# Mixture-of-experts stage on Trainium2: gate and up contracted over 128 rows, then over the two 64-row halves of the array, with the remainder's weights streamed per tile

## What is computed

```python
xf = x.reshape(N, Dv)                       # N = 3072 tokens, Dv = 192, layernormed
logits = xf @ router_w.T
top_logits, top_idx = jax.lax.top_k(logits, 2)
top_w = jax.nn.softmax(top_logits, axis=-1)
for e in range(8):
    w_e = jnp.sum(top_w * (top_idx == e), axis=-1)
    h = jax.nn.silu(xf @ Wg[e].T) * (xf @ Wu[e].T)     # 192 -> 768, twice
    out = out + h @ Wd[e].T * w_e[:, None]             # 768 -> 192
```

## Time and profile before

| | |
|---|---|
| median of 3 runs | 2037.2 us (2034.75 to 2037.57) |
| the profiled execution, own time | 2037.6 us |
| its span in the trace | 2035.9 us |
| Mamba program | 0 to about 1513.5 us |
| routing, first gathers | 1513.5 to 1561 us |
| the 55 tiles | 1561 to 2036 us |
| TensorE busy over the span | 1523.3 us (75%) |
| VectorE busy over the span | 1514.1 us (74%) |

### The profile page before, as it was taken

The page is one execution under the profiler, slowest core; times in us unless marked ns, Lnnn a source line. Parts: engine busy times, 40 slices in busy tenths (PEclk is TensorE's granted clock), DMA queues, the critical chain, the costliest instruction groups (busy, mean ns, idle before and its releaser), DMA issues. The chain is left out here.

```text
span 2035.9 us, 19521 instructions
## 1 busy us (share of the span) xinstructions
PE 1523.3 (75%) x4714; PEld 866.1 (43%) x4715; DVE 1514.1 (74%) x1780; ACT 861.1 (42%) x1848; POOL 1056.5 (52%) x539
## 2 busy tenths in 40 slices
PE   6566776776677677767767775876643899999997
PEld 4233343343344334434433443443332566666665
DVE  3699999999999999999999999999954122222221
ACT  2555545554554555455455454554510222222221
POOL 2465676675667657655675675548600233333332
PEclk8777897888788778878878887888875999999999
DMA  3412303031231303122130402213025411111111
GB/s 80 148 48 79 119 29 136 21 129 52 85 114 35 136 16 133 38 99 97 53 120 18 147 37 100 85 42 136 0 73 133 114 26 24 25 24 24 26 24 22
DMA packets 49182, 144.71 MB, mean 71 GB/s; under 512 B 13118, under 2 KB 26028, under 8 KB 48332
## 3 DMA queue, kind: packets, MB, share of 16 engines
q1 hardware_dynamic: 36956, 129.61, 18.7%
q0 software_dynamic: 12144, 14.30, 4.2%
HBM read 132.67 MB, written 11.21 MB: 71 GB/s over the span
## 5 line engine op out<-in xcount | busy, mean ns | idle before, releaser
L629 POOL TENSOR_TENSOR ring<-dtu,brep 128x1536 f32<-128x1536 f32 x192 | 661.0, 3447 | 446.0 <-DVE states L640 316.3
L652 PE MATMUL py<-ring,ident 128*128 128x384 f32 x1536 | 637.2, 568 | 133.7 <-DVE yg L669 110.5
L640 DVE TENSOR_TENSOR_SCAN states<-states,ring 128x768 f32<-128x768 f32 x384 | 673.7, 1755 | 30.2 <-ACT states L616 14.7
L652 PEld LDWEIGHTS py<-ring,ident 128*128 128x128 f32 x1536 | 332.7, 223 | 420.6 <-issue 186.2
L616 ACT ACTIVATE states<-dt_,aneg 128x376 f32<-128x376 f32 x768 | 406.1, 560 | 0.0
L642 DVE TENSOR_TENSOR ring<-states,crep 128x768 f32<-128x768 f32 x384 | 367.6, 957 | 13.2
L613 ACT ACTIVATE states<-zero_cols 128x16 f32<-128x16 f32 x384 | 71.2, 186 | 642.7 <-DVE ring L642 637.6
L1288 PE MATMUL gu<-w,xsT 96*128 x660 | 298.3, 602 | 7.2 <-issue 6.6
L462 PE MATMUL pf<-xT,wxz 97*128 97x384 f32 (+1 forms) x384 | 183.7, 624 | 139.0 <-ACT xT L449 55.3
L1329 DVE COPY yidx<-place 128x1 int32 (+1 forms) x56 | 8.4, 153 | 250.8 <-DMA out_tokens<-ys,yidx 250.8
L1288 PEld LDWEIGHTS gu<-w,xsT 96*128 96x128 f32 x660 | 122.6, 193 | 145.6 <-issue 145.6
(11 more groups left out here) (221 smaller groups left out, 1412.3 us busy)
## 6 DMA issues: line engine op xcount, KB each, us to landing
brep<-b_c_rows SPq DMA_DIRECT2D x64, 768.0 KB, 4.1
crep<-b_c_rows SPq DMA_DIRECT2D x64, 768.0 KB, 4.6
w<-in_w SPq DMA_DIRECT2D x8, 1152.0 KB, 14.2
wd<-in_wd SPq DMA_DIRECT2D x8, 576.0 KB, 16.3
ptok<-in_p_tok SPq DMA_DIRECT2D x8, 384.0 KB, 3.8
pT<-in_p_T SPq DMA_DIRECT2D x8, 384.0 KB, 4.8
out_tokens<-h SPq DMA_DIRECT2D x8, 288.0 KB, 2.1
x_scratch<-x SPq DMA_DIRECT2D x8, 288.0 KB, 2.9
```

Source lines behind the costliest of these rows:

```text
L629: gp.tensor_tensor(ring[:, w % NRING], dtu[:, d, o, :].unsqueeze(1).to_broadcast([128, GN, T]), brep[:, ng], ALU.mult).then_inc(dbu_ok, 1)
L640: v.tensor_tensor_scan(h_in, h_in, x_in, 0.0, ALU.mult, ALU.add).then_inc(scan_ok, 1)
L652: mm = pe.matmul(py[:, 0:T], ident[:], ring[:, w % NRING, i, :], start=(ng == 0 and i == 0), stop=False)
```

## The change

1. The contraction over 192 features is cut as 128 + 64 instead of 96 + 96. For the first 128 rows there are four matmuls on the full array (512 and 256 columns, for gate and for up). For the last 64 rows gate uses partitions 0 to 63 and up partitions 64 to 127: matmuls of 64 rows, 512 columns of gate, 512 of up, 256 of gate, 256 of up.
2. For that the tile's features 128 to 191 must stand on both halves. The table's rows grow to XR + E = 264 floats, SP stores features 128 to 191 a second time per chunk, the second transpose takes 128 columns, and the gather moves 1056 B a row instead of 800.
3. `w13` becomes 128 partitions by 49152 B (768 KB an expert instead of 1152). The weights of the last 64 rows are loaded for each tile into one of two buffers `rest` (`sp_rest`, 384 KB a tile, on SP's queue, its expert number read by SP). It waits until gate/up of tile j-2 is done. `pe_gu` waits for it between its two parts.
4. On SP's queue the loads for tiles 0 and 1 stand ahead of expert 2's weights, those for tiles 2 to 5 behind the weights of expert 7, the others in a loop.
5. Gate and up start on PSUM banks of their own (`gu` grows to 4 banks); `cnt` shares its bank with `yps`.

```diff
-XW = D + E
+XR = 256
+XW = XR + E
@@ norm_x3, and SP's wait at the program's end
-            wait(eng, x3_out, 16 * c)
+            wait(eng, x3_out, 32 * c)
@@ sp_store
             sp.dma_start(rows_of(rows, c), src[:]).then_inc(done, 16)
+            if what == "x3":
+                sp.dma_start(rows_of(dram["x3"][:, D:XR], c), x3[:, :, 128:D]).then_inc(x3_out, 16)
@@ build_experts
-        w13 = sb("w13", [KH, E, 2, 2 * HF])
+        w13 = sb("w13", [128, E, 2 * HF])
+        rest = sb("rest", [128, 2, HF])
-        xsT = sb("xsT", [KH, 2, 2, 128])
+        xsT = sb("xsT", [128, 2, 2, 128])
-        gu = pb("gu", [128, 2 * HF])
+        gu = pb("gu", [128, 2048])
+        gate_up = [gu[:, 1024 * i:1024 * i + HF] for i in range(2)]
-        cnt = pb("cnt", [128, 512])
+        cnt = yps
@@ pe_xT
-            for k in range(2):
-                mm = pe.transpose(xps[0:KH, 128 * k:128 * k + 128], xs[:, b, KH * k:KH * k + KH], ident[:])
-            mm.then_inc(xt_ps, 1)
+            pe.transpose(xps[:, 0:128], xs[:, b, 0:128], ident[:])
+            pe.transpose(xps[:, 128:256], xs[:, b, 128:XR], ident[:]).then_inc(xt_ps, 1)
@@ new
+        def sp_rest(sp, j, b):
+            wait(sp, gu_ok, j - 1)
+            if not isinstance(j, int):
+                alone(sp)
+            e = sp.value_load(owner[0:1, bass.ds(j, 1)], min_val=0, max_val=E - 1)
+            sp.dma_start(rest[:, b, :], a["w13_rest"][:, bass.ds(e, 1), :].rearrange("p a n -> p (a n)")).then_inc(rest_in[b], 16)
@@ pe_gu
-            for n in range(3):
-                for k in range(2):
-                    mm = pe.matmul(gu[:, 512 * n:512 * n + 512], xsT[:, b, k, :], w13[:, bass.ds(e, 1), k, 512 * n:512 * n + 512].rearrange("p a n -> p (a n)"), start=(k == 0), stop=(k == 1))
+            pieces = ((0, 512), (512, HF))
+            for i in range(2):
+                for lo, hi in pieces:
+                    pe.matmul(gate_up[i][:, lo:hi], xsT[:, b, 0, :], w13[:, bass.ds(e, 1), HF * i + lo:HF * i + hi].rearrange("p a n -> p (a n)"), start=True, stop=False)
+            pe.wait_ge(rest_in[b], 16 * (n + 1))
+            for lo, hi in pieces:
+                for i in range(2):
+                    rows = slice(64 * i, 64 * i + 64)
+                    mm = pe.matmul(gate_up[i][:, lo:hi], xsT[rows, b, 1, :], rest[rows, b, lo:hi], start=False, stop=True)
             mm.then_inc(gu_ok, 1)
@@ SP's queue
             for c in range(NCH):
                 sp.dma_start(rows[c], row_w[:, NT * c:NT * c + NT, :]).then_inc(weights_out, 16)
+            sp.wait_ge(rv.sem, rv.after("owner", 0))
+            sp_rest(sp, 0, 0)
+            sp_rest(sp, 1, 1)
             weights(2)
             for b in range(2):
                 sp.wait_ge(xs_in[b], 16)
             for e in range(3, E):
                 weights(e)
+            for j in range(2, HEAD):
+                sp_rest(sp, j, j % 2)
+            with sp.Fori(0, (NJ - HEAD - 1) // 4) as i:
+                for r in range(4):
+                    sp_rest(sp, 4 * i + HEAD + r, r % 2)
+            sp_rest(sp, LAST, LAST % 2)
```

More of the change, by code:

```diff
@@ L1055, in _ @@
             sp.wait_ge(h2_out, 16 * NCH)
-            sp.wait_ge(x3_out, 16 * NCH)
+            sp.wait_ge(x3_out, 32 * NCH)
             sp.wait_ge(filled, 32)
@@ L1229, in build_experts @@
         xs_in = [sem(f"slot_tile_loaded{b}") for b in range(2)]
+        rest_in = [sem(f"rest_weights_loaded{b}") for b in range(2)]
         xt_ps = sem("slot_tile_transposed")
@@ L1280, in act_xT, with pe_gu @@
             wait(act, gu_ok, j - 1)
-            act.activation(xsT[:, b].rearrange("p k t -> p (k t)"), xps[0:KH, 0:256], ACT.Copy).then_inc(xt_sb, 1)
-        def pe_gu(pe, j, b, e):
+            act.activation(xsT[:, b].rearrange("p k t -> p (k t)"), xps[:, 0:256], ACT.Copy).then_inc(xt_sb, 1)
+        def sp_rest(sp, j, b):
[4 more added lines that the diff above has]
+            sp.dma_start(rest[:, b, :], a["w13_rest"][:, bass.ds(e, 1), :].rearrange("p a n -> p (a n)")).then_inc(rest_in[b], 16)
+        def pe_gu(pe, j, b, n, e):
             pe.wait_ge(xt_sb, j + 1)
             wait(pe, hid_ok, j)
-            for n in range(3):
-                for k in range(2):
-                    mm = pe.matmul(gu[:, 512 * n:512 * n + 512], xsT[:, b, k, :], w13[:, bass.ds(e, 1), k, 512 * n:512 * n + 512].rearrange("p a n -> p (a n)"), start=(k == 0), stop=(k == 1))
+            pieces = ((0, 512), (512, HF))
[7 more added lines that the diff above has]
+                    mm = pe.matmul(gate_up[i][:, lo:hi], xsT[rows, b, 1, :], rest[rows, b, lo:hi], start=False, stop=True)
             mm.then_inc(gu_ok, 1)
@@ L1293, in act_gate @@
             wait(act, hid_ok, j)
-            act.activation(act_g[:], gu[:, 0:HF], ACT.Silu).then_inc(sg_ok, 1)
+            act.activation(act_g[:], gate_up[0], ACT.Silu).then_inc(sg_ok, 1)
         def dve_hid(v, j):
@@ L1298, in dve_hid @@
             wait(v, ht_ps, j)
-            v.tensor_tensor(hid[:], act_g[:], gu[:, HF:2 * HF], ALU.mult).then_inc(hid_ok, 1)
+            v.tensor_tensor(hid[:], act_g[:], gate_up[1], ALU.mult).then_inc(hid_ok, 1)
         def pe_hT(pe, j):
@@ L1332, in dve_weight @@
             v.wait_ge(xs_in[b], 16 * n + 16)
-            v.tensor_tensor(own_w[:, b, :], xs[:, b, D:XW], of_tile[:, bass.ds(j, 1), :].rearrange("p a e -> p (a e)"), ALU.mult).then_inc(own_ok, 1)
+            v.tensor_tensor(own_w[:, b, :], xs[:, b, XR:XW], of_tile[:, bass.ds(j, 1), :].rearrange("p a e -> p (a e)"), ALU.mult).then_inc(own_ok, 1)
             v.wait_ge(own_ok, j + 1)
@@ L1458, in weights @@
             def weights(e):
-                sp.dma_start(w13[:, e].rearrange("p k n -> p (k n)"), a["w13"][:, e, :]).then_inc(w_in[e], 16)
+                sp.dma_start(w13[:, e], a["w13"][:, e, :]).then_inc(w_in[e], 16)
                 sp.dma_start(wd[:, e].rearrange("p k n -> p (k n)"), a["wd"][:, e, :]).then_inc(w_in[e], 16)
@@ L1464, in _ @@
             sp.wait_ge(rv.sem, rv.after("row_w", 0))
-            rows = dram["x3"][0:NTOK, D:XW].rearrange("(c p t) e -> c p t e", c=NCH, t=NT)
+            rows = dram["x3"][0:NTOK, XR:XW].rearrange("(c p t) e -> c p t e", c=NCH, t=NT)
             for c in range(NCH):
                 sp.dma_start(rows[c], row_w[:, NT * c:NT * c + NT, :]).then_inc(weights_out, 16)
+            sp.wait_ge(rv.sem, rv.after("owner", 0))
+            sp_rest(sp, 0, 0)
+            sp_rest(sp, 1, 1)
             weights(2)
@@ L1559, in tile @@
                 e = ahead.pop("expert") if ahead else owner_of(pe, j)
-                pe_gu(pe, j, b, e)
+                pe_gu(pe, j, b, n, e)
                 if follows:
@@ L1582 @@
           "bm_in", "inT", "outw", "bmoT", "xpw_bc", "xpw_dt", "dtw", "dtb", "cw", "cb", "dskip", "a_log",
-          "outb", "ln_g", "ln_b", "rw", "w13", "wd"]
+          "outb", "ln_g", "ln_b", "rw", "w13", "w13_rest", "wd"]
 def fusion_block(nc, a, out):
@@ L1639, in lay_out @@
         "rw": rows(f["L0_ffn_router_w"].T, KH),
-        "w13": np.stack([f["L0_ffn_Wg"], f["L0_ffn_Wu"]], 1).reshape(E, 2, HF, 2, KH).transpose(4, 0, 3, 1, 2).reshape(KH, E, 4 * HF),
+        "w13": np.stack([f["L0_ffn_Wg"], f["L0_ffn_Wu"]], 1)[..., 0:128].transpose(3, 0, 1, 2).reshape(128, E, 2 * HF),
+        "w13_rest": np.stack([f["L0_ffn_Wg"], f["L0_ffn_Wu"]], 1)[..., 128:D].transpose(1, 3, 0, 2).reshape(128, E, HF),
         "wd": f["L0_ffn_Wd"].reshape(E, D, HF // 128, 128).transpose(3, 0, 2, 1).reshape(128, E, (HF // 128) * D),
```

## The result

The changed kernel takes 1976.09 us (median of 4 runs, 1973.64 to 1977.15) against 2037.38; the ratio is 0.9696, 95% interval 0.9683 to 0.971. I had forecast 2013 with a range from 1984 to 2050.

The account below looks back on a forecast made before the run. TensorE was taken to bound the steady tiles at 7.99 us each; 52 tiles x 0.54 us saved made 28, less 4 lost at the start, net 24, hence 2013 us, range 1984 to 2050.

Parts of the forecast that it names:

- The bound: Tiles' steady part: TensorE sets the time, busy 98.41 of 100 us, 7.99 us a tile.
- The full part: Gate/up's full-array matmuls: four records of 512 columns and four of 256 take 2.63 us a tile.
- The remainder: Gate/up's last 64 rows on two halves: staggered overlap from in-order issue, 1.77 us a tile, bounds 1.32 and 2.63.
- My rival of full overlap: Gate/up's remainder: the halves' records pair off, 1.32 us, 0.99 saved a tile, giving 1990 us; chance 0.2.
- The change of shape: TensorE in gate/up: one visit a tile to a smaller row group costs 0.17 us, bounds 0 and 0.35.
- The slot transposes: Transposes between gate/up and down: loading 128 columns instead of 96 adds 0.05 us a tile.
- Sum a tile: Steady tile on TensorE: 0.54 us saved after full part, remainder, change of shape and slot transposes.
- The first tiles: Start of the expert tiles: tile 2 waits for its remainder load behind the weights, +4 us, bounds -3 and +12.
- The scatter's circle: Chain from `ys` through scatter and `hid` over two tiles: 14.2 us, 7.1 a tile, below TensorE's 7.45.
- my third rival: Steady tiles: the remainder's load delays the scatter by 1.6 us, hardly 0.1 saved a tile, 2035 us; chance 0.13.
- Covered parts: Table's second store and wider gathers: hidden, costing nothing; the store's bounds 0 and +2 us in all.
- No overlap: Gate/up's remainder: halves run one behind the other, 2.63 us, 0.32 more a tile, 2058 us; chance 0.22.

Follow-up runs that it names:

- the first experiment: Changed kernel with gate's and up's remainder both on partitions 0 to 63, the array's second half unused: 2042.48 us, ratio 1.003.
- The second experiment: Changed kernel with the remainder's loops exchanged, so all of gate's records stand ahead of up's: 1976.15 us, ratio 0.9701.
- the two-visit kernel: Changed kernel with gate/up cut by columns, so TensorE goes from full array to halves and back twice a tile: 1998.3 us, ratio 0.9813.
- The padded kernel: Kernel before with gate/up weights stored and loaded on 128 partitions instead of 96, the added ones unread copies: 2030.44 us, ratio 0.9963.

## Why the prediction was right in direction and wrong in size

**The bound.** TensorE set the time in the steady part, as read from the earlier trace rows; the first experiment moves it by 66 us with nothing but TensorE's work. Right.

**The full part.** 2.63 forecast, 2.67 measured, of which 0.09 belong to the change of shape. A 256-column record takes 0.215 us, not 0.228. The straight line was good; I had put down's modelled length of 2.12 us on it instead of 1.95, from start to start, with which it gives 0.217. Right within 0.05.

**The remainder: the step that failed.** I took 1.77 us, because "the second must wait for the first; up's first record comes behind gate's second and can only run beside that". The dependence inside one half is real, but it does not hold up the other half. With both halves fed from the start the eight records take 4 x 0.43 / 2 + 4 x 0.215 / 2 = 1.29 us, and 0.20 for the passage: 1.49. No row of before has two row groups in flight, and I chose between the bounds by an assumption about issue order that no row supported. The second experiment shows it false. My rival of full overlap had this term right (1.32), with 1990.

**The change of shape: a term sized too low.** 0.17 a visit forecast. Measured are 0.09 + 0.20 inside gate/up and 0.06 behind it, on the first slot transpose: 0.35, the upper bound of my 0 to 0.35. The second visit of the two-visit kernel cost 0.40. The trace of before had that price. After the earlier trace rows it goes on with

```profile
1495.21 0.59 PE L681 MATMUL pq<-dtw,ones 1*128 1x192 f32 x2
```

From 1492.55 to 1495.21 two one-row records and twelve full ones of the same width take 2.66 us. At down's 1.95 / 12 from start to start they would take 2.28, so the visit cost 0.38. I had looked at the way back alone, and at the rate of the modelled 2.12.

**The slot transposes.** +0.05 forecast, +0.06 measured (0.28 against 0.22), but by luck. The second of them loads 128 columns and takes 0.11 us, as one of 96 columns did before; the extra time lies on the first one and belongs to the change of shape. By starts, the hidden transposes of before, which load 128, also took 0.66 / 6 = 0.11 each: the wider load cost nothing.

**Sum a tile.** 5.16 - 4.16 - 0.06 = 0.94 us instead of 0.54. The remainder's records gave 0.48 more than forecast, the change of shape 0.18 less, and the full part and the slot transposes 0.05 more each. Over 52 tiles that is 21 us of the 37 that I missed; the trace has 51.3 us from tile 3 on, 2.4 more than 52 x 0.94: about 1 of it the slow records of the old gate/up 3, which I had put to the start, and about 0.8 the loop's turn, which costs 0.68 instead of 0.75 us, twelve times.

**The first tiles: the other step that failed.** I forecast +4 and the trace has -6.4. The order of events was right: tile 2 stops for `rest`, TensorE restarts slowly (2.93 us for the remainder), slot transposes and down come behind the stop. But I moved 6.9 MB at the 247 to 268 GB/s of the earlier trace rows, a mean of two kinds of load. The changed layout puts all weights on 128 partitions, and they flow at about 410: the longest landing is 16.1 us. That price was in the trace of before, though not among my rows: the rates inside the window alternate, as shown above, and I had only looked at means over 5 us. From +4 to -6.4 it is 10 us of the 37. The padded kernel shows the rate's part by itself: 5.0 us, although it moves more bytes.

**The scatter's circle.** Forecast with full overlap: 13.8 us for two tiles, 0.1 a tile from being the bound. In the trace `hid` starts at 1707.49, 0.18 after silu has ended, and its transposes start right when down is through. It is that close, and still TensorE's: the transposes' start is set by down's end, 0.17 us behind the end of `hid`. I had named a `hid` that waits for the scatter instead of silu as the sign of my third rival. That sign came and the rival did not hold: a faster gate/up alone brings silu ahead of the scatter's circle, and twice the loads change nothing.

**What is left.** 21 and 10 us leave 6 of the 37: the 2.4 above and 3.3 of the Mamba part, late in the one trace of the kernel before. The medians' difference, 61 us, is no smaller than the spans', although other traces of the unchanged Mamba program are as early; how much of the 61 that part holds in the median stays open.

**Covered parts.** The second store and the wider gathers cost nothing within 2 us, as forecast; they were measured alone. That the shared PSUM bank costs nothing fits the steady tile, which has no term left over, but was not tried by itself.

**No overlap.** Forecast 2058, measured 2042.5 on one half. The size a tile was right (2.78 against 2.63 + 0.17); the difference is the start, where I had +4 and its trace has 10 less (3.3 of it Mamba's).

## What to carry to other kernels

A contraction that does not fill the array can be cut into a full part and a part on two halves, and the halves then do run at once, in both orders of the code that were tried; keep all work of one shape together, since a visit to the other shape and back cost 0.35 to 0.40 us here. Take a record's price from start to start, not from a modelled length, and count both ends of a visit. Where no row shows a mechanism, forecast both ends and say what the trace gives for each; a value between them needs a reason of its own from the trace. And look at a transfer's rate kind by kind before scaling it: a new layout may change the rate more than the bytes.

## What the runs showed of the hardware

- Float32 records on different 64-row halves overlap completely: 1.49 us for eight records on two halves, 2.78 on one, starts 0.01 us apart instead of 0.43.
- The overlap does not depend on neighbours in the code: 1.50 us with four records of one half ahead of four of the other.
- In these traces weight loads do not run ahead across a change of array shape; a passage costs about 0.2 us at 2.4 GHz, half of it behind the first record of the new shape.
- The time of a record from start to start goes with its columns: 0.11 us for 128, 0.163 for 192, 0.215 for 256, 0.43 for 512; loading 96 or 128 columns of weights makes no difference (0.11 us for either transpose).
- Loads from DRAM to 96 partitions ran at about 230 GB/s, to 128 partitions at about 410, and the length of a partition's run (12288 or 6144 B) made none of the difference: a packet of 12288 B took about 820 ns on 96 and 460 on 128, one of 6144 B about 400 and 234.
